# Silu from one table function, a two-tanh forget gate and a new call order in a gated-recurrence plus feed-forward kernel

## The reference, cut to what matters

```python
def attn(x):                       # x: 4 sequences of 512 tokens, 256 features, layer-normed
    q = silu(x @ Wq1 @ Wq2)
    f = sigmoid(x @ Wk1 @ Wk2)
    a = exp(log_sigmoid(f))        # = sigmoid(f), the decay
    v = x @ Wv
    h[s] = a[s] * h[s-1] + (1 - a[s]) * v[s]      # scan over the tokens
    out = q * h
    out = out * rsqrt(mean(out**2) + 1e-6) * norm_w
    return out @ Wo
x = x + layernorm(attn(layernorm(x)))
def ffn(x):                        # 6 blocks, 256 -> 1024 -> 256, float32
    for i in range(6):
        x = gelu(x @ W1[i].T + B1[i]) @ W2[i].T + B2[i] + x
        if i < 5: x = layernorm(x) * LN_G[i] + LN_B[i]
    return x
x = x + layernorm(ffn(layernorm(x)))
```

## Time and profile before

| | us |
|---|---|
| median of 3 runs (lowest to highest) | 627.94 (627.71 to 628.29) |
| the profiled execution | 629.86 |
| its span, first to last instruction | 628.0 |
| TensorE busy | 619.8 (99%), 2893 products |
| VectorE busy | 470.1 (75%) |
| ScalarE busy | 407.9 (65%) |
| GpSimd busy | 250.4 (40%) |

### The profile page before, as it was taken

The page is one execution under the profiler, slowest core; times in us unless marked ns, Lnnn a source line. Parts: engine busy times, 40 slices in busy tenths (PEclk is TensorE's granted clock), DMA queues, the critical chain, the costliest instruction groups (busy, mean ns, idle before and its releaser), DMA issues.

```text
span 628.0 us, 8878 instructions
## 1 busy us (share of the span) xinstructions
PE 619.8 (99%) x2893; PEld 516.4 (82%) x2893; DVE 470.1 (75%) x820; ACT 407.9 (65%) x688; POOL 250.4 (40%) x232
## 2 busy tenths in 40 slices
...
GB/s 285 62 47 0 1 2 0 4 17 88 38 38 40 10 64 6 5 36 38 42 33 5 40 39 2 72 7 4 37 40 38 36 5 6 5 4 76 119 106 103
DMA packets 56877, 25.13 MB, mean 40 GB/s; under 512 B 47360, under 2 KB 52864, under 8 KB 56832
## 3 DMA queue, kind: packets, MB, share of 16 engines
...
...
## 4 chain that ended last, share of the span: by engine, by line
PE 92%; DVE 3%; issue 2%; ACT 2%; POOL 1%; POOLq 0%; DVEq 0%; ACTq 0%
PE BK L169 47%; PE BK L351 38%; PE BK L301 3%; PE BK L175 1%; PE BK L366 1%; PE BK L198 1%; DVE OL L534 1%; PE BK L242 0%; POOL X L1188 0%; ACT R L835 0%; PE BK L262 0%; PE BK L253 0%; PE BK L254 0%; PE BK L232 0%; ACT R L849 0%
## 5 line engine op out<-in xcount | busy, mean ns | idle before, releaser
L945 ACT ACTIVATE HH<-BK,B 128x512 fp32r<-128x512 f32 x192 | 132.1, 688 | 140.5 <-PE BK L169 136.2
L563 DVE TENSOR_TENSOR HL<-BK,HH 128x512 fp32r<-128x512 f32 x192 | 130.7, 683 | 83.3 <-ACT BK L951 82.8
L169 PE MATMUL BK<-XH,WL 128*128 128x512 f32 x416 | 162.5, 391 | 0.7 <-DVE HL L563 0.7
L169 PE MATMUL BK<-XL,WH 128*128 128x512 f32 x416 | 162.1, 390 | 0.0
L169 PE MATMUL BK<-XH,WH 128*128 128x512 f32 x416 | 162.0, 389 | 0.0
L351 PE MATMUL BK<-HH,WL 128*128 128x512 f32 x368 | 143.7, 390 | 0.0
L351 PE MATMUL BK<-HH,WH 128*128 128x512 f32 x368 | 143.2, 389 | 0.0
L351 PE MATMUL BK<-HL,WH 128*128 128x512 f32 x368 | 143.2, 389 | 0.0
L951 ACT ACTIVATE BK<-BK,B 128x512 f32<-128x512 f32 x192 | 125.8, 655 | 0.0
L169 PEld LDWEIGHTS BK<-XH,WL 128*128 128x128 f32 x416 | 78.1, 188 | 17.3 <-DVE HL L563 1.1
L169 PEld LDWEIGHTS BK<-XH,WH 128*128 128x128 f32 x416 | 78.1, 188 | 16.5
...
## 6 DMA issues: line engine op xcount, KB each, us to landing
STG<-in_w SPq DMA_DIRECT2D x24, 512.0 KB, 3.9
...
X<-in_x SPq DMA_DIRECT2D x3, 512.0 KB, 8.2
R<-turns SPq DMA_DIRECT2D x3, 512.0 KB, 4.1
...
sums<-P SPq DMA_DIRECT2D x40, 8.0 KB, 1.4
R<-in_wv SPq DMA_DIRECT2D x1, 512.0 KB, 6.5
```

The costliest lines, as they stand in the source:

```text
L169: r = eng.matmul(dst, s, m, start=i == 0, stop=i == len(todo) - 1)
L563: eng.tensor_tensor(HL[:, g % HR, :], bank["mm1", n, j][:, :], HH[:, g % HR, :].bitcast(f32), ALU.subtract).then_inc(S["hlo"], 1)
L945: eng.activation(HH[:, g % HR, :], bank["mm1", n, j][:, :], ACT.Gelu, bias=B1[:, 8 * (n // 4) + j:8 * (n // 4) + j + 1]).then_inc(S["ghi"], 1)
```

## The change

It does five things.

- `silu(t, m)` replaces `tq` and `q` in tiles 0 and 1: ScalarE makes the silu in one instruction of the function Silu, from PSUM into QB. VectorE's `q` (L505) is gone there, eight instructions, and the bank of `zq` is free when `silu` is done. `warm()` loads the table set with Silu in place of Sigmoid. A second table load stands at `gelu_in()` as before.
- In tiles 0 and 1 `t1` and `t2` are two tanh, as in tiles 2 and 3. `kv` reads KB. The affine step that makes AB from KB is `decay(t, m)`, a GpSimd instruction on 128x512 elements, eight in all; it waits for `t2` and for the scan two groups back. `scan` of these tiles waits for `decay`.
- Tiles 2 and 3 keep their functions.
- Four semaphores of constants become one, `consts`.
- The hand-written lists of all engines are in a new order, both those ahead of the loop and those behind it. The number of products and their shapes are as before.

```diff
-                freed[b] = S["q"], 4 * t + m + 1
+                freed[b] = (S["silu"], 4 * t + m + 1) if t < SILU else (S["q"], 4 * (t - SILU) + m + 1)
...
-                if t < 2:
-                    ve.wait_ge(S["a"], 4 * t + m + 1)
-                else:
-                    ve.wait_ge(S["t2"], 4 * (t - 2) + m + 1)
-                eng.scalar_tensor_tensor(vb[:, :], (AB if t < 2 else KB)[:, p, :], -1.0, vb[:, :],
-                                         ALU.add, ALU.mult).then_inc(S["kv"], 1)
+                ve.wait_ge(S["t2"], 4 * t + m + 1)
+                eng.scalar_tensor_tensor(vb[:, :], KB[:, p, :], -1.0, vb[:, :], ALU.add, ALU.mult).then_inc(S["kv"], 1)
...
+            def silu(t, m):
+                i = 4 * t + m
+                ac.wait_ge(S["zq"], i + 1)
+                gate_free(i)
+                eng.activation(QB[:, m, :], bank["zq", t, m][:, :], ACT.Silu).then_inc(S["silu"], 1)
...
-                if t < 2:
-                    eng.activation(FB[:, :], bank["zk", t, m][:, :], ACT.Sigmoid).then_inc(S["t1"], 1)
-                else:
-                    eng.activation(FB[:, :], bank["zk", t, m][:, :], ACT.Tanh, scale=0.5).then_inc(S["t1"], 1)
+                eng.activation(FB[:, :], bank["zk", t, m][:, :], ACT.Tanh, scale=0.5).then_inc(S["t1"], 1)
...
+            def decay(t, m):
+                i, p = 4 * t + m, m % 2
+                po.wait_ge(S["t2"], i + 1)
+                if i >= 2:
+                    po.wait_ge(S["scan"], i - 1)
+                eng.tensor_scalar(AB[:, p, :], KB[:, p, :], 0.5, 0.5, ALU.mult, ALU.add).then_inc(S["decay"], 1)
```

Further on in TensorE's list, between `rms(3)` and `turn3(3, 0)` (the transposes of tile 3 for the feed-forward stage), there stood ten units `mm1` or `mm2`; now there stand twelve, and the unit `mm2(1, 3)`, which stood between `proj(3, 3)` and `rms(3)`, has given way to `turn3(2, 1)`, `mm1(1, 5)` and `mm1(1, 6)`:

```diff
-            mm1(1, 6, 3); proj(3, 3); mm2(1, 3); rms(3, 2); mm1(1, 7, 0); mm2(1, 4); mm2(1, 5); mm2(1, 6)
-            mm1(2, 0, 1); mm2(1, 7); mm1(2, 1, 2); mm1(2, 2, 3); mm2(2, 0); mm1(2, 3, 0); turn3(3, 0, 1)
+            proj(3, 3); turn3(2, 1, 0); mm1(1, 5, 1); mm1(1, 6, 3); rms(3, 2); mm1(1, 7, 0); mm1(2, 0, 1); mm2(1, 4)
+            mm2(1, 5); mm2(1, 6); mm1(2, 1, 2); mm1(2, 2, 3); mm2(1, 7); mm2(2, 0); mm1(2, 3, 0); mm2(2, 1); mm2(2, 2)
+            turn3(3, 0, 1); turn3(3, 1, 2); mm1(2, 4, 3); mm2(2, 3); mm1(2, 5, 1); mm1(2, 6, 2); mm1(2, 7, 0)
```

More of the change, by code:

```diff
@@ L26 @@
 ldb1 ldb2 ldlg ldlb ldp0 ldp1 put1 got1 put2 got2 away0 away1 away2_0 away2_1 away3 half_tokens tokens0 tokens1
-tokens2 tokens_last stored one mhalf quarter half eps idle_in nw sel wq1_hi wk1_hi wq2_hi wk2_hi wv_hi wo_hi wq1_lo
+tokens2 tokens_last stored one consts idle_in nw sel wq1_hi wk1_hi wq2_hi wk2_hi wv_hi wo_hi wq1_lo
 wk1_lo wq2_lo wk2_lo wv_lo wo_lo wo_scaled bias wp_hi wp_lo f_st f_mv f_ve f_rs f_nm l1_st l1_mv l1_ve l1_ng l1_rs
 l1_nb l1_nm l2_st l2_mv l2_ve l2_ng l2_rs l2_nb l2_nm x1 l3_st l3_mv l3_ve l3_ng l3_rs l3_nb l3_nm turn1 turn3
-xhi1 xlo1 xhi3 xn xlo3 xhi xlo up u uhi ulo zq tq q zk t1 t2 a v kv scan o ohi osq olo proj ssum sq_turn sq_part
+xhi1 xlo1 xhi3 xn xlo3 xhi xlo u uhi ulo zq tq q silu zk t1 t2 decay a v kv scan o ohi osq olo proj ssum sq_turn sq_part
 rms ms mm1 ghi gf hlo mm2 y sum1 tr1 red1 tot1 mub ctr sqr sum2 tr2 red2 tot2 vae rsd rsb nn res swap swap_last pre
@@ L378, in _ @@
[L378 to L387, removed]
@@ new lines, in _ @@
+            v(2, 1, 4); zk(2, 1, 3); proj(1, 3); mm1(0, 0, 1); mm1(0, 1, 2); rms(1, 3); mm1(0, 2, 0); zq(2, 3, 3)
+            mm1(0, 3, 1); mm1(0, 4, 2); mm2(0, 0); mm2(0, 1); zk(2, 2, 0); mm1(0, 5, 3); mm2(0, 2); proj(2, 0)
+            proj(2, 1); turn3(1, 0, 1); turn3(1, 1, 2); v(2, 2, 0); mm2(0, 3); mm1(0, 6, 1); turn1(3, 0, 2)
+            turn1(3, 1, 3); mm2(0, 4); up(3, 0, 2); up(3, 1, 0); u(3, 0); mm1(0, 7, 3); u(3, 1); zk(2, 3, 1)
+            proj(2, 2); zq(3, 0, 1); zq(3, 1, 2); v(2, 3, 3); mm2(0, 5); zk(3, 0, 1); v(3, 0, 2); zk(3, 1, 1)
@@ new lines, in _ @@
+            l2_st(1, 3); l2_mv(1, 1); q(2, 2); hlo(0, 0); l2_mv(1, 2); l2_mv(1, 3); ms(1); kv(2, 1); hlo(0, 1)
+            scan(2, 1); o(2, 0); o(2, 1); l3_st(1, 0); hlo(0, 2); l3_st(1, 1); l3_mv(1, 0); l3_st(1, 2); q(2, 3)
+            l3_mv(1, 1); l3_mv(1, 2); l3_st(1, 3); l3_mv(1, 3); olo(2, 0); olo(2, 1); hlo(0, 3); hlo(0, 4); xlo3(1, 0)
+            xlo3(1, 1); kv(2, 2); hlo(0, 5); scan(2, 2); xlo1(3, 0); o(2, 2); xlo1(3, 1); hlo(0, 6); ulo(3, 0)
+            olo(2, 2); sel(); hlo(0, 7); ulo(3, 1); q(3, 0); q(3, 1); kv(2, 3); scan(2, 3); o(2, 3); kv(3, 0)
```

286 lines of the change are left out of this document (146 added, 140 removed).

## The result

| | before | changed kernel |
|---|---|---|
| median (lowest to highest), us | 627.88 (627.71 to 628.29) | 635.53 (634.91 to 636.34) |
| the profiled execution, us | 629.86 | 636.34 |
| its span, us | 628.0 | 634.5 |
| ratio of the medians, 95% interval | | 1.0122 (1.0104 to 1.0139) |

What follows compares the result with a forecast made beforehand. TensorE, busy 619.8 of 628.0 us, was taken as the bound, with some 3.3 us of losses to regain. +0.2 and −0.75 us gave −0.55, so 627.4 us from a median of 627.94; range 626.0 to 629.4.

Steps and rivals of the forecast that it cites:

- The sum: Whole kernel: +0.2 us in the first tile and −0.75 us from 42 to 150 us, together −0.55 us.
- Rival (c): Near 166 us: rsd(0), behind two more weight-splitting pieces, delays hlo(2, 7) and bank 0; 1.6 us lost, 629.0; 10 in 100.
- Term 1: Tiles 0 and 1: VectorE loses 5.4 us of q; silu 0.59, t2 0.72, decay 0.9 us; of itself TensorE unmoved.
- Term 2: First tile: ScalarE waits at wp_hi(1) for weights; TensorE loses 1.63 us against 1.43 us lost before: +0.2 us.
- Term 3: From 42 to 150 us: old waits of 1.05 us go, 0.3 us of new ones come: −0.75 us.
- Term 4: The end: the wait ahead of 596.47 us stays, through a bank shared by two products; change zero.
- (a): First tile: ScalarE's wait at wp_hi(1) does not bite; 1.55 us less, 625.9; 12 in 100.
- (b): First part: GpSimd and VectorE obstruct each other, each such olo costing 1.03 us; two give 629.2; 10 in 100.
- The hold: First tile: ScalarE stands still 1.8 us at wp_hi(1) until weights land at 17.08 us; TensorE waits about 1.45 us.
- Rival (d): No new waits from 42 to 150 us and a first tile that comes out even: 626.7; 8 in 100.

Runs made afterwards that it cites:

- old_first_new_rest: The kernel before up to 62 us, then the changed kernel's order on every engine, end included: 1.0090 of the kernel before, 634.41 us.
- new_first_old_rest: The changed kernel's functions and order for what it issues in the first 62 us, then the order of the kernel before: 1.0018 of the kernel before.
- old_tuned: The kernel before with turn3(3, .) behind mm2(2, 1) and banks 0 and 1 exchanged in mm1(23, .): 0.9976 of the kernel before.

## Why the prediction was wrong, point by point

**The sum had no term between 150 and 300 us.** This is the step that failed. I took the losses of before as the stock and asked which would go; where before had none, I looked for new ones only at a few places and called the stretch unchanged. Of the 7.65 us, 5.5 lie there (old_first_new_rest); the trace has 6.7. I had seen that the new list moves norm 0's `tr2(0)` and `red2(0)` behind `hlo(1, 7)`, but did not follow `put2(0)` into SP's queue, because its list is the same. Its times were not.

**Rival (c) had the place and the victim, but neither cause nor size.** It said: bank 0 of `mm1(3, 3)`, near 166 us, through `hlo(2, 7)`. That is where the longest wait stands, 2.9 us. But `rsd(0)` was done at 162.8 and `tot1(1)` ended last, 2.7 us later; moving `rsd(0)` ahead changed nothing for VectorE, moving `ldp(7)` took all away. And I gave it 10 in 100 and 1.6 us, without the three waits that follow. The sign that I had named for it, a wait of over 1 us for HL near 166 us, came, and did not tell the two causes apart: had the time come out near (c), that would have been luck.

**Term 1 was right.** The groups of after by line and form, to 60 us, beside the earlier trace rows:

```profile
L1218 POOL TENSOR_SCALAR AB<-KB 128x512 f32<-128x512 f32 x8 | 5.4, 678 | 3.3 <-ACT KB L921 3.2
...
L921 ACT ACTIVATE KB<-FB,QU 128x512 f32<-128x512 f32 x9 | 6.5, 720 | 0.0
L896 ACT ACTIVATE QB<-BK 128x512 f32<-128x512 f32 x8 | 4.6, 591 | 0.4 <-PE BK L170 0.3
```

`silu` 0.59 and `t2` 0.72 as taken; `decay` 0.68 in the mean, inside 0.53 to 1.30, where I took 0.9. Seven of the eight took 0.62 us and one 1.08. The Trainium skill (GPSIMD Engine Reference, 3.1 Elementwise) had 0.44 to 0.77 and the dispatch, by an estimate from its cycles; the trace agrees for the seven, and it was nearer than the middle of my rows.

**Term 2 had the mechanism and, in half of the traces, the size.** ScalarE and TensorE after:

```profile
16.35 1.06 ACT L824 ACTIVATE WH<-STG 128x1024 fp32r<-128x1024 f32 x1 [1.22 <-DMA STG<-in_w]
...
22.55 1.58 ACT L837 ACTIVATE R<-X,NBS,RS 128x256 f32<-128x256 f32 x3
```

```profile
24.27 1.06 PE L233 MATMUL BK<-ID,R 128*128 128x128 f32 x8 [0.78 <-ACT R L837]
```

The last `l1_nm` ends at 24.13, 7.8 us behind the start of `wp_hi(1)`, and 7.8 was the sum I had made. In this execution the weights landed 0.75 us earlier than in the earlier trace rows, so the loss was 0.9 us and not 1.63; in new_first_old_rest it was 1.7. Of the eight traces with this beginning four have 1.5 us idle there, the others 0.8 to 1.3. The waits at 30.85 and 32.66 went as forecast, and one of 0.47 us for OL came at 36.09. What I mis-sized is the exchange: +0.2 forecast, 1.4 measured by the medians, of which 1.1 to 1.3 went with the move of `wp_hi(1)`. I had set 1.63 against the 1.43 lost in one execution of before that was itself 1.9 us above its median. The new order ties the first tile to the moment a transfer lands: in new_first_old_rest TensorE reached its first `zq` 1.0 us ahead of the profiled execution of before (11.23 and 12.26), and at the transposes of tile 1 nothing of that was left (25.06, and 25.02 in the earlier trace rows). That the ordinary executions of before keep such a lead is inferred, since only one of them has a trace, and the later medians of before (628.9 to 629.6 us) lie close to that execution's 629.86.

**Term 3 was right up to its edge.** The waits at 126.64 and 148.56 have no counterpart, small new ones came (0.19 us at 104, 0.16 at 129), and from 40 to 150 us TensorE lost 1.5 us instead of 2.2: −0.7 where I had −0.75. That the two agree so well is partly luck, since I had counted only 1.05 of the 2.2. The dense list that gave this back is the list that put norm 0 late.

**Term 4 was right for the wait near 596 us** (0.70 us idle at 602.44, 0.69 before), and old_tuned shows that the shared bank was its cause, as I had said. The 0.6 us more at 619.79 I did not foresee; they go with four slow DMA issues, and why these are slow is open.

**Rivals (a) and (b).** The hold bit in every trace of the new beginning, so (a) did not happen. As for (b), no `olo` ahead of 33 us took over 0.8; one took 1.57 us at 34.47, beside GpSimd, and cost the 0.47 us at 36.09, and one took 1.72 at 54.7 and cost nothing. The prices of (b) were real and rare.

**Rival (d)** has a slip in its sum: with a first tile that comes out even and no new waits the change is −1.05 us, which gives 626.9 and not 626.7. Nothing hangs on it.
